# Another order of the same operations on five engines of an attention, FFN and spiking layer

## What is computed

```python
xn = layernorm(x)
# attention
h = layernorm(xn) * ln_scale + ln_bias
c_q, c_kv = h @ w_down_q.T, h @ w_down_kv.T                # 64 latents each
q, k, v = c_q @ w_up_q.T, c_kv @ w_up_k.T, c_kv @ w_up_v.T # 16 heads of 64
q, k = rope(q), rope(k)
attn = softmax(q @ k.T / 8)
a = (attn @ v) @ w_out.T + xn
# feed-forward and spikes
y = square(relu(xn @ W_fc.T)) @ W_proj.T
for _ in range(5):                                         # mem starts at 0
    mem = 0.9 * mem + y - (mem > 1); spikes += mem > 1
out = x + a + spikes / 5
```

## Time and profile before

| what | value |
|---|---|
| median of 3 runs | 1187.81 us (1187.14 to 1190.89) |
| profiled execution | 1185.65 us, span on the core 1183.8 us |
| busy: PE, ACT, DVE, POOL | 1001.8, 923.8, 900.7, 895.0 us |
| TensorE clock granted | 0.99 of full speed over the span |
| DMA | 217.96 MB, mean 184 GB/s, queue 1 takes 68.7% of 16 engines |
| chain that ended last, largest shares | issue 27%, SP's queue 26%, POOL 21% |

### The profile page before, as it was taken

The page is one execution under the profiler, slowest core; times in us unless marked ns, Lnnn a source line. Parts: engine busy times, 40 slices in busy tenths (PEclk is TensorE's granted clock), DMA queues, the critical chain, the costliest instruction groups (busy, mean ns, idle before and its releaser), DMA issues.

```text
span 1183.8 us, 25999 instructions
## 1 busy us (share of the span) xinstructions
PE 1001.8 (85%) x6880; PEld 734.1 (62%) x6880; DVE 900.7 (76%) x1223; ACT 923.8 (78%) x3008; POOL 895.0 (76%) x897
## 2 busy tenths in 40 slices
PE   3669888888888898888889888889888888988967
PEld 2546666666666666666666666666666666666644
DVE  3687878877778787787888777878778787877852
ACT  3678787888887888878787888888788888878751
POOL 3657977877887887787787788778778778778831
PEclk9899999999999999999999999999999999999989
DMA  5277667767776766776776677677677677767770
GB/s 165 90 199 210 173 189 204 180 190 197 194 191 187 202 181 189 212 178 190 199 184 187 191 203 186 191 196 186 188 206 186 187 194 188 191 185 199 202 173 24
DMA packets 93281, 217.96 MB, mean 184 GB/s; under 512 B 22464, under 2 KB 43200, under 8 KB 93120
## 3 DMA queue, kind: packets, MB, share of 16 engines
q1 hardware_dynamic: 92864, 216.52, 68.7%
q10 hardware_dynamic: 384, 1.05, 0.4%
HBM read 7.77 MB, written 4.19 MB: 10 GB/s over the span
## 4 chain that ended last, share of the span: by engine, by line
issue 27%; SPq 26%; POOL 21%; DVE 7%; PE 7%; DMA 6%; ACT 5%; POOLq 1%; ACTq 1%; DVEq 0%
SPq L255 25%; POOL partner L884 10%; POOL u_sb L928 6%; ACT prob L561 4%; DVE turned L740 4%; DMA x_sb<-in_x 3%; DMA resid<-early 3%; POOL qk L887 2%; PE ps_b L449 2%; POOL rstd L899 1%; DVE qk L724 1%; PE ps_u L343 1%; POOL early L910 1%; PE ps_qk L317 1%; PE ps_s L327 1%
## 5 line engine op out<-in xcount | busy, mean ns | idle before, releaser
L561 ACT ACTIVATE prob<-ps_s,neg_max 128x256 f32<-128x256 f32 x1024 | 474.3, 487 | 27.6 <-DVE neg_max L729 27.6
L884 POOL TENSOR_TENSOR partner<-partner,rope_sb 128x512 f32<-128x512 f32 x256 | 327.5, 1279 | 166.9 <-DMA partner<-raw 166.9
L740 DVE STREAM_TRANSPOSE turned<-prob 128x1024 f32<-128x1024 f32 x256 | 316.2, 1235 | 111.0 <-ACT prob L561 109.3
L887 POOL TENSOR_TENSOR qk<-qk,partner 128x512 f32<-128x512 f32 x256 | 325.8, 1273 | 20.1
L729 DVE TENSOR_REDUCE neg_max<-ps_s 128x4 f32<-128x1024 f32 x256 | 299.9, 1200 | 4.6 <-PE ps_s L327 4.6
L327 PE MATMUL ps_s<-qk 64*128 64x256 f32 x2048 | 267.7, 395 | 32.3 <-ACT prob L561 24.4
L573 ACT COPY raw<-ps_qk 128x512 f32<-128x512 f32 x256 | 150.2, 587 | 152.1 <-PE ps_qk L318 147.8
L327 PEld LDWEIGHTS ps_s<-qk 64*128 64x128 f32 x2048 | 188.2, 187 | 108.6 <-issue 75.6
L343 PE MATMUL ps_u<-gathered,ckv 128*64 128x256 f32 x2048 | 251.7, 388 | 0.0
L561 ACT ACTIVATION_READ_ACCUMULATOR prob<-ps_s,neg_max 128x1 f32 x1024 | 223.2, 218 | 0.0
L317 PE MATMUL ps_qk<-latent,wup_hi 128*128 128x256 f32 x512 | 166.8, 348 | 42.7 <-DVE qk L724 39.5
(11 more groups left out here) (67 smaller groups left out, 880.7 us busy)
## 6 DMA issues: line engine op xcount, KB each, us to landing
gathered<-turned SPq DMA_DIRECT2D x1016, 128.0 KB, 2.3
partner<-raw SPq DMA_DIRECT2D x256, 256.0 KB, 2.4
x_sb<-in_x SPq DMA_DIRECT2D x32, 128.0 KB, 2.1
resid<-early SPq DMA_DIRECT2D x32, 128.0 KB, 2.0
out<-out_sb SPq DMA_DIRECT2D x32, 128.0 KB, 2.0
turned<-in_wup SPq DMA_DIRECT2D x2, 512.0 KB, 5.8
gathered<-turned ACTq DMA_DIRECT2D x8, 128.0 KB, 4.9
rope_sb<-in_rope SPq DMA_DIRECT2D x1, 512.0 KB, 6.9
```

What stands on the lines that cost most here:

```text
L561: last = nc.scalar.activation(prob[:, s % 2, :, h, :, t, :].rearrange("p j k c -> p k j c"), ps_s[:, s % 2, h, t, :].rearrange("p (k j c) ...
L740: nc.vector.transpose(turned[:, par, :, s % GROUP, :], prob[:, s % 2, :, :, :, :, :].rearrange("p j h k t c -> p j (h k t c)"))\
L884: nc.gpsimd.tensor_tensor(other, other, sin_sb, ALU.mult).then_inc(sin_ready, 1)
L887: nc.gpsimd.tensor_tensor(qk[:, s % RING, :, :], qk[:, s % RING, :, :], other, ALU.add).then_inc(rope_done, 1)
```

## The change

No instruction is added or taken away in a batch; `step` of every engine is written anew as four cases, one for each quarter. The functions that `step` calls are as before. Letters: b is the batch of the quarter.

SP's stream (of the whole diff the part that concerns DMAs):

```diff
-                if q == 0 and not outside(b + 1, B) and not outside(b + 3, B):
-                    sp.wait_ge(res_ready, done(b + 1))
-                    load_x(b + 3, 1 - b0)
-                if not outside(g + LEAD["project"], STEPS):
-                    exchange(i * BODY + ahead, ahead)
-                if last % GROUP == GROUP - 1 and not outside(i * BODY + last, STEPS):
-                    move(...)
-                if q == 1:
+                if q == 0:
+                    if raws:
+                        exchange(i * BODY + ahead, ahead)
+                elif q == 1:
                     if not outside(b - 2, B):
                         store(b - 2, b0)
                     if not outside(b, B):
                         sp.wait_ge(res_ready, done(b))
                         keep_residual(b0)
+                    if raws:
+                        exchange(i * BODY + ahead, ahead)
+                    if last % GROUP == GROUP - 1 and not outside(i * BODY + last, STEPS):
+                        move(...)
+                elif q == 2:
+                    if raws:
+                        exchange(i * BODY + ahead, ahead)
+                else:
+                    if not outside(b + 2, B) and not outside(b + 4, B):
+                        sp.wait_ge(res_ready, done(b + 2))
+                        load_x(b + 4, b0)
+                    if raws:
+                        exchange(i * BODY + ahead, ahead)
+                    if last % GROUP == GROUP - 1 and not outside(i * BODY + last, STEPS):
+                        move(...)
```

A few lines of the other engines:

```diff
 POOL, quarters 0 and 1
-                if not outside(g + LEAD["rope"], STEPS):
-                    for k in range(2):
-                        add_rotated(g + LEAD["rope"] + k, s + LEAD["rope"] + k, i)
-                if q < 3 and spread:
-                    normalise_u(b - 1, (0, 2, 3)[q], 1 - b0)
+                if q == 0:
+                    add_rotated(g + ahead, s + ahead, i)
+                    normalise_u(b - 1, 0, 1 - b0)
+                    add_rotated(g + ahead + 1, s + ahead + 1, i)
+                    normalise_u(b - 1, 1, 1 - b0)
+                elif q == 1:
+                    inverse_std(b + 3)
+                    normalise_u(b - 1, 2, 1 - b0)
+                    add_rotated(g + ahead, s + ahead, i)
+                    add_rotated(g + ahead + 1, s + ahead + 1, i)
+                    split_sums(b)
...
```

More of the change, by code:

```diff
@@ L672, in step @@
                         copy_rden(b - 1)
+                    if raws:
+                        copy_projected(g + far, s + far, i)
+                    if exps:
+                        exponentials(g + near, s + near, i)
+                    if not outside(b + 1, B) and not outside(b + 2, B):
+                        lead_latents(b + 2, b0)
+                    if not outside(b + 1, B):
+                        copy_latents(b + 1, 1 - b0)
+                    if exps:
+                        exponentials(g + near + 1, s + near + 1, i)
@@ L679, in step @@
                     if not outside(b + 3, B):
                         normalise(b + 3, 1 - b0, 1)
-                if raws:
-                    copy_projected(g + LEAD["project"], s + LEAD["project"], i)
-                if q < 2 and spread:
-                    copy_spread(b - 1, 2 * q)
-                if q == 3 and not outside(b + 1, B):
-                    relu(b + 1, 1)
-                if q == 0 and isinstance(b, int) and b == -1:
-                    copy_value_by_output()
-                if exps:
-                    exponentials(g + LEAD["scores"], s + LEAD["scores"], i)
@@ new lines, in step @@
+                    if turns:
+                        row_max(g + near + 1, s + near + 1)
+                    if not outside(b + 1, B) and not outside(b + 3, B):
+                        moments_of(b + 3, 1 - b0, i + 1 + b0)
+                    if turns:
+                        turn(g + near, s + near, i)
+                    if not outside(b + 1, B) and not outside(b + 2, B):
+                        split_latents(b + 2, b0)
+                    if rotates:
+                        rotate(g + far + 1, s + far + 1)
```

372 lines of the change are left out of this document (235 added, 137 removed).

## The result

| kernel | median | ratio to before | profiled span |
|---|---|---|---|
| before | 1187.47 us (1185.59 to 1190.89) | 1 | 1183.8 us |
| changed | 1060.81 us (1059.56 to 1063.33) | 0.8933 (95% 0.8906 to 0.896) | 1057.8 us |

The page of the changed kernel: span and busy time, which answer to the earlier trace rows, and the two lines of the chain that ended last.

A forecast was written before the change was run, and what follows sets the result against it. The prediction took one loop of waits through SP, POOL, PE, ACT and DVE as the bound. Gains of 103.5 (steady batches), 2.5 (last half-batches) and 0 (start and end) made 106 us, 1187.8 to 1081.8, stated as 1083; range 1052 to 1143.

The forecast's parts named there:

- The loop: Quarter 3's move on SP, quarter 0's exchange, POOL, PE, ACT, DVE, next move: 34.66 us a batch, falling to 27.6.
- The load's term: On SP, loading x ahead of exchange and move instead of between them takes 0.58 us out of the loop.
- POOL's own work: On POOL, pairs, chunks, inverse deviations, split and residual make 29.3 us a batch; 1.0 lost on a spread copy makes 30.3.
- The chain of exponentials: Through ACT and DVE, last exponential to last exponential over four quarters: 8.0, 8.2, 7.4 and 6.9, 30.5 us a batch.
- The allowance of 0.8 us: Added to 30.5 us a batch for two or three tight meetings between queues missed by 0.3 us each, giving 31.3.
- the steady term: Gain over 28.5 batches, each falling from 34.93 to 31.3 us: 103.5 us.
- The last half-batches: Last three half-batches, without loads of x or inverse deviations, fall from 49.47 to 47 us: 2.5 gained.
- Start and end: Ramp and tail, including the moved setup product and swapped matmul groups, each priced at 0, between -2 and +2 us.
- the forecast's own case: Whole kernel at 31 to 32.3 us a batch, 1062 to 1100 us in all; chance 51%.
- Everything meets: Rival in which no tight meeting between queues is missed: 30.5 us a batch, 1059 us in all; chance 20%.
- The rule on the shared port: DVE transpositions locking out POOL could add 9.9 us a batch; priced at 0, given no chance of its own.
- One sign of being wrong: On SP, standing waiting for POOL's residual before loading x would show the prediction wrong; no size given.

The follow-up runs named there:

- chunks_alone: The kernel before with two of POOL's chunks moved: chunk 2 ahead of quarter 1's pairs, chunk 3 ahead of quarter 2's; 1142.1 us, ratio 0.9623.
- act_less: The changed kernel with POOL's four chunks and ACT's four spread copies half as wide (output differs); 1050.08 us, 30.65 us a batch.
- pe_less: The changed kernel with PE's weighted latents over half of the tokens, 8 of 16 matmuls a quarter left out; 1055.61 us, 31.03 us a batch.
- pool_less: The changed kernel with POOL's chunks half as wide, half of the normalisation left out; 1060.81 us, 31.08 us a batch.
- quarter3_old: The changed kernel with ACT's second projected copy between quarter 3's exponential blocks again and DVE's rotation between the transpositions; 1065.96 us, 31.31 us a batch.
- setup_old: The changed kernel with the one-time setup product of values and output weights back in its old place on PE and ACT; 1065.55 us, 31.09 a batch.
- pe_order_old: The changed kernel with PE's old step order; 1242.35 us, ratio 1.0464, 36.97 us a batch.
- x_path_old: The changed kernel with x's old path: load behind the move, moments in quarter 1, inverse deviations and normalisations later; 1146.36 us, 33.94 us a batch.
- spread1_moved: The changed kernel with PE's old order, except chunk 1's spread matmul in its new place and quarter 1's order following it; 1071.95 us, 31.40 a batch.

## Why the prediction was right, step by step

- **The loop.** Right. With SP's and POOL's steps alone 3.05 of 3.83 us a batch went. The load's term, 0.58, measured 0.55. The statement that this loop is the only one near 34.7 us was incomplete: chunks_alone met a second one, move, load of x, DVE, at 33.18. The change opens both, so it cost the forecast nothing; that is luck, for the prediction had only one chain as tight.
- **POOL's own work, 30.3 us.** The wait for the spread copy was put at 1.0 us and is 1.07. But pool_less shows that the term is no bound, and the prediction took 30.3 as a lower one: POOL still waits for the exchange.
- **The chain of exponentials, 30.5 us.** Of the chains that were tested it is the one that decides (act_less against pe_less and pool_less). That its links simply add up is too strong: the 1.5 us that quarter3_old was to put into it cost 0.23. Between the ends of the last exponentials of quarters 3, 0, 1, 2 and 3 (589.4, 597.4, 605.8, 613.3, 620.4) I read 8.0, 8.4, 7.45 and 7.15; predicted were 8.0, 8.2, 7.4 and 6.9. The rows of ACT in the two intervals that came out longer, with their waits, are the second spread copy, the first projected copy and the relu of quarter 3:

```profile
600.01 0.58 ACT L623 COPY spread<-ps_b 128x512 f32<-128x512 f32 x1 [0.51 <-POOL u_sb L1034]
...
615.51 0.58 ACT L610 COPY raw<-ps_qk 128x512 f32<-128x512 f32 x1 [1.15 <-PE ps_qk L330]
616.29 0.60 ACT L664 ACTIVATE relu_sb<-ps_a 128x512 f32<-128x512 f32 x1 [0.20 <-PE ps_a L397]
```

- **The allowance of 0.8 us.** 0.58 was needed, 31.08 against 30.5. The rows above fit the reason given, meetings missed by some tenths, but no run tests it. With 31.3 for 31.08 the steady term was 103.5 and is 109.9 us.
- **The last half-batches.** 2.5 predicted, 4.3 measured.
- **Start and end, the mis-sized term.** Priced at 0 within 2 us, they gave 7.0 + 4.8 = 11.8. The reason that I gave, that PE waits in those stretches anyway, was the reason why it pays: work that moves into a gap leaves a later place free. Of the ramp setup_old explains 4.2 us, its lower clock included. For the other 2.8 and the end's 4.8 there was no run of its own. In the end PE bears part of the time: pe_less is 4.4 us shorter there.
- **The sum.** 103.5 + 2.5 + 0 against 109.9 + 4.3 + 11.8 = 126.0. Half of the 22 us between 1083 and 1060.81 is start and end.
- **The rivals.** The time, 1060.81, stands 1.2 us outside the 1062 to 1100 of the forecast's own case and 1.8 from the 1059 of *Everything meets*. The batch does not: 31.08 us is in the forecast's 31 to 32.3 and above that rival's 30.5. The time came near it through start and end, which were priced at 0; that it lies so close is luck.
- **The rule on the shared port.** The Trainium skill, SBUF — State Buffer (SBUF: two separate sides), has GpSimd and VectorE locking each other out in some kinds of instruction. By the row of the changed kernel (min/median/max ns) the price stays 0, with DVE busy 86% of the time:

```profile
L990 POOL TENSOR_TENSOR partner<-partner,rope_sb x256: 1262/1277/1297, 22.3 to 1011.6; 128x512 f32<-128x512 f32 x128
```

- **The signs named.** Moves 31.3 apart: 31.03. POOL's wait under 60 us: 46.3. The new one before chunk 0, 1 us a batch: 1.07 in the batch shown, 50.5 us in all with one of 15.2 among its 30. DVE's wait for x gone: from 33.5 to 3.0, and that one is in the ramp. PE's wait for chunk 3 gone. POOL and ACT above 85%: 84.7% and 86.8%. One sign of being wrong was wrong itself: SP does wait for the residual before it loads x, 34.8 us in 28 waits (in the batch shown POOL's `early` ends at 620.10, the load starts at 620.28), yet the exchange behind it had nothing to send before 621.5, when ACT's copy ended.
- **Expectations that missed later.** pe_order_old and quarter3_old were priced from the waits of one engine, with the others' order held to be free. In both an engine's old order met another's new one. chunks_alone, x_path_old and pe_less missed as well (34.3, 32.8 and 30.5 to 30.8 us a batch expected, 33.18, 33.94 and 31.03 measured): the signs held, the sizes of single parts did not.

## What to carry to other kernels

With in-order queues, first follow the cycle that closes once an iteration through all engines and DMA queues, and price a reordering by what leaves this cycle; full engines may still wait, so test a bound by cutting its work (3.0 us a batch less on PE gave 0.05 here, 0.83 less on ACT gave 0.43). The orders of the engines are one schedule: with one engine's old order among the others' new ones a batch took 36.97 us, more than with all old (34.91) or all new (31.08). And price ramp and tail by their gaps: the setup product, 3.6 us long, was worth 4.7 us in one.

## What I had not expected of the hardware

A single wait of PE, repeated in every batch, brings its clock down. In pe_order_old PE stands still for 4.08 us ahead of one matmul. Behind it the granted clock is 0.50, the lower of the two levels (1.2 instead of 2.4 GHz), and sixteen matmuls take 3.68 us that take 1.95 elsewhere in the batch. With the wait gone (spread1_moved) the granted clock is 0.99 again, and PE is busy 1.9 us a batch less.

In the ramp both levels stand in every version, at other times. A group of eight score matmuls shows them, in the kernel before and twice in the changed one:

```profile
41.06 2.08 PE L327 MATMUL ps_s<-qk 64*128 64x256 f32 x8 [2.26 <-ACT prob L561]
```

```profile
38.95 1.14 PE L339 MATMUL ps_s<-qk 64*128 64x256 f32 x8 [1.57 <-ACT prob L598]
...
46.69 2.08 PE L339 MATMUL ps_s<-qk 64*128 64x256 f32 x8 [0.88 <-ACT prob L598]
```

PE had waited shortly before each of them, for exponentials and, between projections, for DVE. Which of these waits brings the clock down, these runs don't tell apart.

Splitting sixteen score matmuls into two groups of eight, with a projection between them, made them 0.2 us longer by their starts (2.13 against 1.93), with no idle time shown; one place of one trace shows it.
